# Three products of an expert unit on GpSimd instead of two, with one more ScalarE step, in a small vision tower on Trainium2

## The reference

```python
x_glu = jnp.minimum(x_glu, LIMIT)                 # LIMIT = 7
x_lin = jnp.clip(x_lin, -LIMIT, LIMIT)
return x_glu * jax.nn.sigmoid(ALPHA * x_glu) * (x_lin + 1.0)
```

## Time and profile before

| what | value |
|---|---|
| median of 3 runs | 711.4 us (709.51 to 711.79) |
| the profiled execution's own time | 711.66 us |
| its span, first to last instruction | 709.9 us |
| PE busy / PEld busy | 599.4 us (84%) / 503.3 us (71%) |
| DVE busy | 491.3 us (69%) |
| ACT busy | 276.3 us (39%) |
| POOL busy | 381.4 us (54%) |
| mean granted TensorE clock | 0.885 |

### The profile page before, as it was taken

The page is one execution under the profiler, slowest core; times in us unless marked ns, Lnnn a source line. Parts: engine busy times, 40 slices in busy tenths (PEclk is TensorE's granted clock), DMA queues, the critical chain, the costliest instruction groups (busy, mean ns, idle before and its releaser), DMA issues.

```text
span 709.9 us, 10373 instructions
## 1 busy us (share of the span) xinstructions
PE 599.4 (84%) x3341; PEld 503.3 (71%) x3341; DVE 491.3 (69%) x937; ACT 276.3 (39%) x684; POOL 381.4 (54%) x437
## 2 busy tenths in 40 slices
PE   4656856689899999879999987899998799986996
PEld 4445745568688888757888875788786678865774
DVE  1152575368987676898877789889869985555664
ACT  1262266225454423525443352554333333222332
POOL 3332467353756443557754546577655574462664
PEclk8557777859589999879999997899999899997999
DMA  7915232650035323104522230354432155261862
GB/s 205 338 47 199 90 111 90 217 226 1 0 96 161 124 89 146 66 7 121 177 88 97 98 131 13 93 147 153 147 107 78 40 173 171 99 228 39 263 225 74
DMA packets 41826, 88.34 MB, mean 124 GB/s; under 512 B 9580, under 2 KB 34476, under 8 KB 35500
## 3 DMA queue, kind: packets, MB, share of 16 engines
q1 hardware_dynamic: 41772, 87.68, 37.9%
HBM read 77.24 MB, written 10.40 MB: 123 GB/s over the span
## 4 chain that ended last, share of the span: by engine, by line
PE 32%; DVE 16%; issue 6%; DMA 4%; ACT 4%; POOL 2%; SPq 1%; POOLq 0%; DVEq 0%; ACTq 0%
PE post L636 8%; PE sums L636 6%; PE gate_up L636 5%; PE linear_up L636 5%; PE y_sum L636 4%; DVE state L1127 4%; PE pre L636 4%; DMA w<-w_store 3%; DVE scratch L1247 3%; DVE scratch L1240 2%; ACT scratch L892 2%; DVE fills L1118 1%; POOL scratch L1360 1%; ACT a_bar L892 1%; SPq L577 1%
## 5 line engine op out<-in xcount | busy, mean ns | idle before, releaser
L1341 POOL TENSOR_TENSOR read<-state,c_all 128x504 f32<-128x504 f32 (+1 forms) x120 | 146.0, 1220 | 140.3 <-DVE state L1127 112.9
L1127 DVE TENSOR_TENSOR_SCAN state<-a_bar,fills 128x504 f32<-128x504 f32 (+1 forms) x120 | 132.5, 1105 | 17.2 <-ACT a_bar L892 15.4
L1360 POOL TENSOR_TENSOR scratch<-scratch 128x252 f32<-128x252 f32 (+1 forms) x120 | 83.8, 698 | 107.7 <-DVE scratch L1247 93.8
L636 PE MATMUL y_sum<-read,ident 128*128 128x252 f32 (+1 forms) x480 | 133.8, 409 | 0.0
L892 ACT ACTIVATE scratch<-scratch 128x252 f32<-128x252 f32 (+1 forms) x120 | 47.4, 395 | 170.4 <-DVE scratch L1240 170.2
L636 PE MATMUL sums<-hid,w 128*128 128x252 f32 (+1 forms) x480 | 104.6, 381 | 9.4 <-POOL hid L1369 9.3
L636 PEld LDWEIGHTS y_sum<-read,ident 128*128 128x128 f32 x480 | 96.3, 218 | 15.8 <-issue 6.0
L892 ACT ACTIVATE a_bar<-dts,decay 128x245 f32<-128x245 f32 (+1 forms) x240 | 100.0, 470 | 0.7 <-DVE state L1127 0.7
L636 PE MATMUL gate_up<-t_high,w 128*128 128x252 f32 (+1 forms) x360 | 89.0, 317 | 12.8 <-DVE scratch L1240 8.6
L1369 POOL TENSOR_TENSOR hid<-scratch,route_rows 128x252 f32<-128x252 f32 (+1 forms) x120 | 85.7, 714 | 13.1 <-DMA route_rows<-mix_rows 6.2
L1247 DVE TENSOR_SCALAR scratch<-scratch 128x252 f32<-128x252 f32 (+1 forms) x120 | 60.5, 504 | 43.8 <-ACT scratch L892 43.1
(11 more groups left out here) (144 smaller groups left out, 895.2 us busy)
## 6 DMA issues: line engine op xcount, KB each, us to landing
w<-w_store SPq DMA_DIRECT2D x40, 1152.0 KB, 5.5
route_rows<-mix_rows SPq DMA_DIRECT2D x192, 63.0 KB, 2.9
w_store<-w SPq DMA_DIRECT2D x8, 1152.0 KB, 5.1
scratch<-expert_w SPq DMA_DIRECT2D x16, 384.0 KB, 5.8
w<-expert_w SPq DMA_DIRECT2D x1, 2304.0 KB
route_rows<-mix_rows SPq DMA_DIRECT2D x48, 36.0 KB, 2.7
w_embed<-embed_w SPq DMA_DIRECT2D x3, 256.0 KB, 3.9
x_patch<-patches SPq DMA_DIRECT2D x1, 756.0 KB, 5.1
```

The source lines that it names most:

```text
L636: return nc.tensor.matmul(out, lhsT, rhs, start=start, stop=stop, skip_group_check=shared)
L1127: dve.tensor_tensor_scan(pair(state, i, c), pair(a_bar, i, c), pair(fills, i, c), 0.0, ALU.mult, ALU.add).then_inc(scanned.sem, 1)
L1341: pool.tensor_tensor(by_state(pair(read, i, c)), by_state(pair(state, i, c)), c_all[:, n:n + 2, 0:tok(c)], ALU.mult).then_inc(read_out.sem, 1)
L1360: pool.tensor_tensor(glu[:, 0:tok(c)], g_act[:, 0:tok(c)], l_clip[un % 2][:, 0:tok(c)], ALU.mult)\
```

## The change

`x_act` on DVE is taken out. ACT gets `x_one` after each `x_tanh`: g_one = g_tanh + 1, into two new buffers, with an Identity activation whose bias is a column of ones. POOL gets `x_gated` ahead of `x_glu`: glu = g_min * l_clip; `x_glu` then is glu = glu * g_one, in place; `x_scale` stays. So POOL makes three products per unit, and DVE two bounds. The waits move with them: `x_tanh` waits for `x_one` of the unit before; `x_one` for `x_tanh` and for `x_glu` two units back; `x_gated` for `x_min`, `x_clip` and the `x_scale` of the unit before; `x_glu` for `x_gated` and `x_one`; `x_min` and `x_clip` for `x_gated` two units back. No DMA is added, removed or moved.

```diff
-        first, second = [("x_gate", un)], [("x_linear", un), ("x_min", un), ("x_tanh", un)]
+        first, second = [("x_gate", un)], [("x_linear", un), ("x_min", un), ("x_tanh", un), ("x_one", un)]
         if un:
-            first += [("x_copy", un - 1), ("x_act", un - 1), ("x_clip", un - 1), ("x_glu", un - 1)]
+            first += [("x_copy", un - 1), ("x_clip", un - 1), ("x_gated", un - 1), ("x_glu", un - 1)]
             second += [("x_scale", un - 1)]
...
-        scratch = sb("scratch", [P, max(9 * TM, 3 * 2 * HALF)])
+        scratch = sb("scratch", [P, max(10 * TM, 3 * 2 * HALF)])
...
-        l_raw, g_tanh, g_act, glu = (piece(0), piece(1)), piece(2), piece(3), piece(4)
-        g_min, l_clip = (piece(5), piece(6)), (piece(7), piece(8))
+        l_raw, g_tanh, glu = (piece(0), piece(1)), piece(2), piece(3)
+        g_min, l_clip, g_one = (piece(4), piece(5)), (piece(6), piece(7)), (piece(8), piece(9))
...
             def x_tanh(c, un):
                 act.wait_ge(gate_min.sem, gate_min.at(c, un + 1))
                 if un:
-                    act.wait_ge(gate_act.sem, gate_act.at(c, un))
+                    act.wait_ge(g_one_ready.sem, g_one_ready.at(c, un))
...
+            def x_one(c, un):
+                act.wait_ge(g_tanh_ready.sem, g_tanh_ready.at(c, un + 1))
+                if un >= 2:
+                    act.wait_ge(glu_ready.sem, glu_ready.at(c, un - 1))
+                activate(g_one[un % 2][:, 0:tok(c)], g_tanh[:, 0:tok(c)], ACT.Identity, bias=ones[:, 0:1])\
+                    .then_inc(g_one_ready.sem, 1)
...
             def x_min(c, un):
                 if un >= 2:
-                    dve.wait_ge(gate_act.sem, gate_act.at(c, un - 1))
+                    dve.wait_ge(gated.sem, gated.at(c, un - 1))
...
             def x_clip(c, un):
                 if un >= 2:
-                    dve.wait_ge(glu_ready.sem, glu_ready.at(c, un - 1))
+                    dve.wait_ge(gated.sem, gated.at(c, un - 1))
...
-            def x_act(c, un):
-                dve.wait_ge(g_tanh_ready.sem, g_tanh_ready.at(c, un + 1))
-                if un:
-                    dve.wait_ge(glu_ready.sem, glu_ready.at(c, un))
-                dve.scalar_tensor_tensor(g_act[:, 0:tok(c)], g_tanh[:, 0:tok(c)], 1.0, g_min[un % 2][:, 0:tok(c)],
-                                         ALU.add, ALU.mult).then_inc(gate_act.sem, 1)
...
-            def x_glu(c, un):
-                pool.wait_ge(gate_act.sem, gate_act.at(c, un + 1))
+            def x_gated(c, un):
+                pool.wait_ge(gate_min.sem, gate_min.at(c, un + 1))
                 pool.wait_ge(linear_clip.sem, linear_clip.at(c, un + 1))
                 if un:
                     pool.wait_ge(hid_ready.sem, hid_ready.at(c, un))
-                pool.tensor_tensor(glu[:, 0:tok(c)], g_act[:, 0:tok(c)], l_clip[un % 2][:, 0:tok(c)], ALU.mult)\
+                pool.tensor_tensor(glu[:, 0:tok(c)], g_min[un % 2][:, 0:tok(c)], l_clip[un % 2][:, 0:tok(c)], ALU.mult)\
+                    .then_inc(gated.sem, 1)
+
+            def x_glu(c, un):
+                pool.wait_ge(gated.sem, gated.at(c, un + 1))
+                pool.wait_ge(g_one_ready.sem, g_one_ready.at(c, un + 1))
+                pool.tensor_tensor(glu[:, 0:tok(c)], glu[:, 0:tok(c)], g_one[un % 2][:, 0:tok(c)], ALU.mult)\
                     .then_inc(glu_ready.sem, 1)
```

More of the change, by code:

```diff
@@ L141, in expert_turns @@
     last = UNITS - 1
-    unit_turns += [[("x_copy", last), ("x_act", last), ("x_clip", last), ("x_glu", last)], [("x_scale", last)]]
+    unit_turns += [[("x_copy", last), ("x_clip", last), ("x_gated", last), ("x_glu", last)], [("x_scale", last)]]
     turns = [[("x_logits", 0)], [("x_topk", 0)], [("x_exp", 0)] + unit_turns[0],
-             [("x_route", 0), ("x_min", 0), ("x_tanh", 0)], [("x_turn", 0)], [("x_mix", 0)],
+             [("x_route", 0), ("x_min", 0), ("x_tanh", 0), ("x_one", 0)], [("x_turn", 0)], [("x_mix", 0)],
              [("x_linear", 0)], [("x_start", 0)]] + unit_turns[2:]
@@ L283, in vit_tower @@
         ident = sb("ident", [P, P])
-        ones = sb("ones", [HM, P])
+        ones = sb("ones", [P, P])
         after_wait = sb("after_wait", [HM, 1])
@@ L476, in vit_tower @@
         g_tanh_ready = signal("g_tanh_ready", UNITS)
-        gate_act = signal("gate_act", UNITS)
+        g_one_ready = signal("g_one_ready", UNITS)
+        gated = signal("gated", UNITS)
         glu_ready = signal("glu_ready", UNITS)
@@ L1026, in _ @@
                  "square3": square3, "t_high": t_high_copy, "x_exp": x_exp, "x_mix": x_mix, "x_copy": x_copy,
-                 "x_tanh": x_tanh})
+                 "x_tanh": x_tanh, "x_one": x_one})
         @block.vector
@@ L1284, in _ @@
                  "t_low": t_low_rest, "x_topk": x_topk, "x_route": x_route, "x_min": x_min, "x_clip": x_clip,
-                 "x_act": x_act, "x_finish": x_finish})
+                 "x_finish": x_finish})
         @block.gpsimd
@@ L1387, in _ @@
             run({"scale": scale, "power": power, "power2": power2, "power3": power3, "split_w1": split_w1,
-                 "drive": drive, "read": read_states, "outproj": outproj, "scale3": scale3, "x_glu": x_glu,
+                 "drive": drive, "read": read_states, "outproj": outproj, "scale3": scale3, "x_gated": x_gated, "x_glu": x_glu,
                  "x_scale": x_scale})
```

## The result

The changed kernel takes 733.0 us (median of 4 runs, 732.5 to 735.4) against 711.2 us of the kernel before in the same comparison: a ratio of 1.032, 95% interval 1.029 to 1.035. The forecast was 732, slower. Two single executions of later runs (813.1 us of gated_on_dve and 786.4 of two_act) had a granted clock of 0.70 and 0.71 instead of 0.88 or 0.89, and are left out of all medians and ratios.

A forecast was written before the change was run, and what follows sets the result against it. PE was taken to set the pace through most of the kernel, with POOL becoming the last cut's bound after the change. Terms 7.8 + 1.7 + 9 + 2 = 20.5 on 711.66 gave 732 us, range 717 to 750.

The forecast's parts named there:

- Last cut: Last cut's expert units, no scan beside them: POOL becomes the bound, 2.48 us per unit against 2.14, 23 intervals, +7.8 us.
- a clip can share a gap that is there anyway: POOL's time per unit: `x_clip` fits into existing gaps between products, so 2.48 us was taken, not 2.77.
- Flush: Five expert units without a scan ahead of the last `scale3`: run at the last cut's pace, +1.7 us (+1.3 to +3.1).
- Dense parts: Three scan starts beside full-rate experts of two cuts back: POOL's work plus `x_one` add +9 us (0 to +18).
- POOL's floor: Dense parts: POOL's busy time, gaps and added products need 108.7 us against 104.1, +4.6 if POOL never waits.
- x_one's loop: Dense parts: `x_one` between tanh and decays lengthens a 3.47 us scan step to 3.96; for a third of 27 steps, +4.5.
- The bound has passed to POOL and ACT: Dense parts: DVE gets room without `x_act`, but POOL and ACT bound; with the rest taken as 0, at best -3.
- Ends of cuts: Last unit of a cut: its chain has one product more, on the path at some cut ends, +2 us (0 to +4).
- Elsewhere: Outside the dense parts: `x_one` is behind PE's work and costs nothing, except where PE waits for `x_copy`.
- Packs well: Rival: POOL's gaps shrink to 0.08, dense parts lose little, cut ends hide; +9.3, 721 us; chance 0.23.
- full lock: Rival: every `x_clip` stops POOL for its whole 0.28 us, 2.77 per unit; +37, 749 us; chance 0.15.
- faster: Rival: POOL products under 0.71 us each, last cut at PE's 1.95 per unit, dense parts gain; -15, 696 us; chance 0.06.

The follow-up runs named there:

- gated_on_dve: The changed kernel with `x_gated` on DVE right behind `x_clip`, `x_one` still ahead of `x_copy`, POOL at two products: 757.3 us, 1.064.
- two_act: The kernel before with a second g_act buffer, so `x_act` waits for the `x_glu` of two units back: 710.1 us, 0.998.
- no_clip: The changed kernel without `x_clip`; the two bounds on the linear half are left out and `x_gated` reads l_raw: 721.4 us, 1.017.
- one_alone: The kernel before plus `x_one` ahead of `x_copy`, its result unread; `x_act` stays on DVE, POOL keeps two products: 720.4 us, 1.014.
- one_behind_copy: The changed kernel with `x_one` moved behind the `x_copy` of the same unit in ACT's order: 721.6 us, 1.014.
- no_one: The changed kernel without `x_one`; `x_tanh` writes the two buffers itself, POOL keeps three products: 722.0 us, 1.015.

## Why the prediction was right in its sum, and where its steps were off

**Last cut, +7.8.** Right in mechanism: POOL's 2.49 us is the sum of the rows, and it alone gives +8.3 (no_clip). Measured +9.3: mis-sized by the 2.60 of the first eight intervals (0.9 us), and by the one of 2.90 (0.4). The step that failed is "a clip can share a gap that is there anyway": in this cut the clip costs POOL's products nothing, but it waits for `x_scale`, `x_min` queues behind it, and the loop through ACT with `x_one` in it closes. I had put `x_one` into the scan's loop and not into this one.

**Flush, +1.7.** Measured +2.4 for five units, by the same two loops; +1.5 with x_one behind `x_copy`.

**Dense parts, +9, of which +4.6 POOL's floor and +4.5 x_one's loop.** Measured +5.4, and the split was wrong. The x_one half is real and was too small: +6.1 in one_alone, and 5.4 + 2.0 = 7.4 when x_one moves behind `x_copy`. (The parts hold 24 `advance` steps, 7, 12 and 5, and not 27; `x_one` takes 0.51, and not 0.41.) The POOL half is not there as an added cost: with the product alone the parts get shorter. POOL does bound them then, but its sum is 99.9 us in a stretch of 102.2, where the forecast's floor was 108.7. The step that failed is to make a floor of every instruction at its old length and of work that POOL need not have finished at the end of a dense part: 112 instructions fall into the parts, not 87 + 30, the last `read` is 2.7 us later there and nobody in the scan waits for it, and `x_scale`, rid of `x_act` beside it, is shorter. "The bound has passed to POOL and ACT" thus held, and left out that taking `x_act` off DVE gives POOL time too. The upper end, 122 us, counted the gaps twice: 77.7 us of work and 30 products of 0.72, at 89% busy, make 112.

**Ends of cuts, +2.** Measured +2.0, but not by the product on the path; that the number fits is luck. More than half of it lies behind the last `x_scale`, 6.62 us instead of 5.52. There PE runs its last eight matmuls, before and then changed, in the columns of the earlier trace rows:

```profile
704.35:706.10 1.75, 1.69 (x8) 0.88 (x8) 0.00 (x0) 0.00 (x0) 0.00 (x1) 1.00 0.00 0
724.69:727.53 2.84, 2.78 (x8) 1.23 (x8) 0.00 (x0) 0.00 (x0) 0.00 (x1) 0.57 0.00 0
```

The granted clock is 1.00 (2.4 GHz) in the first and 0.57, mostly the lower level (1.2 GHz), in the second, and that makes the 1.1 us. PE had idled 3.25 us ahead of them, against 1.74; but in one_alone, without a third product, the same matmuls take 2.98 us after 1.92 idle. Why the clock fell earlier is open. The other 0.9, between the cuts, single executions can't tell from nothing: one_behind_copy, with the same three products, is 0.4 shorter there than the kernel before.

**Elsewhere, 0.** Wrong in two places. One is +3.7 from the last `advance` to the flush, where POOL's backlog and `roots` behind three products delay the norms. The forecast counted what waits behind `x_gated` in the scan (`read`), and not the small POOL steps of `after_scan`. The other is +1.9 in the first units of cut 0: it is `x_one`'s (+1.7 in one_alone, +0.2 with `x_one` behind `x_copy`), where the forecast said that outside the dense parts it costs nothing.

So misses of 1 to 4 us cancelled: -3.6 in the dense parts against +1.5, +0.7, +3.7 and +1.9, with -1.0 and -2.3 in two stretches where single executions differ as much. That the slowdown is mostly POOL's third product and `x_one`'s place was forecast; that the total came within 1 us is luck.

**The rivals.** "Packs well" was right that POOL adds little in the dense parts (its +1 stands against -2.0 with the product alone), but had neither `x_one`'s share there nor the last cut. The full lock fell: in the changed kernel's last cut POOL's products stay at 0.72 beside a waiting clip, in no_one some take 0.80 to 0.82, and clips cost 1.0 us in the last cut. The Trainium skill, SBUF — State Buffer, section "Who interferes with whom", says that whoever issues first holds the shared port pair and the other blocks. The rows agree as to who waits, and show why the price was small: `x_gated` waits for `x_clip`, and in the changed kernel's last cut every clip starts beside a POOL instruction already under way, so it is DVE that pays, mostly 0.83 or 0.72 instead of 0.28. For "faster" the point of decision, 0.71 us per product, was not reached, and its pace of 1.95 for the last cut had another limit than PE: even with POOL going at 1.70 in two_act the cut took 2.10 per unit, by PE's waits for weights.

**The signs named ahead.** DVE fell to 436 us as forecast; POOL rose to 456, not 465; `x_glu` to `x_glu` came out at 2.49 to 2.60 but for one of 2.90, inside the bracket, but with idle time put down to DVE in the first units; POOL over 90% in the dense parts did not come, and its 84% told that something else, `x_one`'s loop, held them in the changed kernel.

## What to carry to other kernels

Where engines run fixed orders, ask of an added step not how long it takes but what stands behind it in the queue: half a microsecond per unit on an engine 45% busy cost some 11 us ahead of `x_copy` and nothing measurable behind it. A product moved to a slack engine is free where another engine sets the pace and costs its time in stretches where its own engine's queue is on the path, so change the form by stretch. And when a floor is summed up from busy time and gaps, check whether the work has to end inside the stretch at all, and whether its instructions keep their length when their neighbour is gone.

## What the runs showed of the hardware that was not expected

- A `x_clip` that takes 0.28 to 0.29 us alone took 0.83 and 0.72 beside a POOL product, and ended 0.14 us after it each time, half its own length; the POOL product kept its 0.72. Where the clip started first (9 units of no_one), the POOL product took 0.80 to 0.82.
- The same product of two 128x252 tiles takes 0.42 us on DVE (gated_on_dve) and 0.72 on POOL.
- `x_one`, an Identity activation with a bias column, takes 0.51 us where `x_tanh` takes 0.41 and `x_copy`, from PSUM, 0.45.
- With two buffers (two_act) the last cut took 2.10 us per unit although POOL could go at 1.70: a weight pair took 6.6 us to land and served three units. That nothing but the weights holds it there was not tried.
- The eight matmuls at the end of the kernel took 1.69 us at a granted clock of 1.00 and 2.78 at 0.57.
